# Attention, RWKV and feed-forward layer on one core: new opening, rings and order, clamps on ScalarE, one product for gain and row scale, and sums as accumulating DMAs

## What is computed

```python
x = x + attention(ln(x))          # q = h @ W_q.T; (q @ h.T) @ h, no softmax
x = x + ffn(ln(x))                # f1
x = x + rwkv(ln(x))
x = x + ffn(ln(x))                # f2, the same weights

def ffn(t):                       # the router's weight is 1 for expert 0
    z = t + relu(t @ w1 + b1) @ w2 + b2
    return ln(z) * gamma + beta

def rwkv(x):
    xa = ln(x) * g1 + b1n; xx = shift(xa)                 # shift: one token later
    k, v, r = (mix of xa and xx with mix_k, mix_v, mix_r) @ Wk, Wv, Wr
    x = x + (sigmoid(r) * wkv(decay, first, k, v)) @ Wo   # a running maximum, two running sums over tokens
    xc = ln(x) * g2 + b2n; xx2 = shift(xc)
    kv = square(relu(mix(xc, xx2) @ FWk)) @ FWv
    return x + sigmoid(mix(xc, xx2) @ FWr) * kv
```

## Time and profile before

| | |
|---|---|
| median of 3 runs | 297.18 us (295.85 to 297.45) |
| the profiled execution | 295.44 us, span 293.6 us |
| TensorE busy | 264.2 us (90% of the span) |
| VectorE busy | 246.4 us (84%) |
| ScalarE busy | 218.7 us (74%) |
| GpSimd busy | 141.2 us (48%) |
| mean granted TensorE clock | 0.973 |

### The profile page before, as it was taken

The page is one execution under the profiler, slowest core; times in us unless marked ns, Lnnn a source line. Parts: engine busy times, 40 slices in busy tenths (PEclk is TensorE's granted clock), DMA queues, the critical chain, the costliest instruction groups (busy, mean ns, idle before and its releaser), DMA issues.

```text
span 293.6 us, 5283 instructions
## 1 busy us (share of the span) xinstructions
PE 264.2 (90%) x1538; PEld 192.0 (65%) x1538; DVE 246.4 (84%) x776; ACT 218.7 (74%) x427; POOL 141.2 (48%) x273
## 2 busy tenths in 40 slices
PE   5378999999999997499899999899999988999990
PEld 5376776678677677266666675696477564867760
DVE  1478369999999999889999999999999999883233
ACT  2369759865999494859999969739979597778630
POOL 1547659725990555726227025637476244431311
PEclk9599999999999999789999999999999999999998
DMA  6921310202220031131022204101400222403031
GB/s 178 300 52 31 60 23 1 36 0 38 36 40 0 0 54 21 17 69 24 1 37 38 36 0 74 36 1 20 90 1 2 36 36 36 112 1 74 0 71 36
DMA packets 14716, 12.59 MB, mean 43 GB/s; under 512 B 1120, under 2 KB 11232, under 8 KB 14688
## 3 DMA queue, kind: packets, MB, share of 16 engines
q0 software_dynamic: 3456, 6.29, 12.6%
q1 hardware_dynamic: 11232, 5.97, 7.1%
HBM read 3.87 MB, written 2.10 MB: 20 GB/s over the span
## 4 chain that ended last, share of the span: by engine, by line
PE 40%; DVE 24%; ACT 12%; issue 12%; POOL 5%; SPq 3%; DMA 2%; POOLq 0%; DVEq 0%; ACTq 0%
PE bank L898 10%; PE bank L883 9%; PE bank L940 6%; PE bank L946 4%; DVE R L383 2%; PE bank L844 2%; ACT KK L738 2%; DMA R<-in_hidden 2%; PE bank L957 2%; PE bank L928 2%; ACT N L632 1%; ACT NC L632 1%; DVE f_zn_stats L332 1%; DVE tmix_stats L332 1%; PE bank L890 1%
## 5 line engine op out<-in xcount | busy, mean ns | idle before, releaser
L898 PEld LDWEIGHTS bank<-W,f_h 128*128 128x128 f32 x512 | 60.1, 192 | 6.6 <-ACT f_h L692 3.5
L898 PE MATMUL bank<-W,f_h 128*128 128x128 f32 x512 | 62.7, 276 | 0.8 <-ACT f_h L692 0.8
L883 PE MATMUL bank<-f_yT,W 128*128 128x512 f32 x128 | 62.0, 601 | 0.7 <-ACT f_yT L684 0.7
L692 ACT ACTIVATE f_h<-bank,B1C 128x512 f32<-128x512 f32 x64 | 42.5, 681 | 14.7 <-PE bank L883 13.4
L946 PEld LDWEIGHTS bank<-FWv,KK 128*128 128x128 f32 x256 | 31.0, 192 | 6.9 <-ACT KK L742 3.1
L883 PEld LDWEIGHTS bank<-f_yT,W 128*128 128x128 f32 x128 | 21.8, 190 | 19.7 <-issue 13.5
L940 PE MATMUL bank<-XK,FWk 128*128 128x512 f32 x64 | 32.4, 620 | 0.6 <-DVE XK L507 0.5
L946 PE MATMUL bank<-FWv,KK 128*128 128x128 f32 x256 | 31.9, 276 | 0.6 <-ACT KK L742 0.5
L632 ACT ACTIVATE f_y<-R,f_yn_nb,f_yn_rs 128x128 f32<-128x128 f32 x64 | 26.3, 486 | 4.6 <-POOL f_yn_nb L252 4.6
L247 POOL TENSOR_TENSOR f_yn_ve<-f_yn_mv,K_EPS 128x4 f32<-128x4 f32 x16 | 4.5, 282 | 43.4 <-DVE f_yn_mv L360 43.4
L297 POOL DMA_DIRECT2D R<-BETA x16 | 15.4, 963 | 20.5 <-ACT f_y L632 20.2
(11 more groups left out here) (131 smaller groups left out, 610.2 us busy)
## 6 DMA issues: line engine op xcount, KB each, us to landing
R<-BETA POOLq DMA_DIRECT2D x16, 256.0 KB, 3.4
R<-in_hidden SPq DMA_DIRECT2D x8, 256.0 KB, 5.0
R<-N POOLq DMA_DIRECT2D x8, 256.0 KB, 3.4
out_x<-R SPq DMA_DIRECT2D x8, 256.0 KB, 2.3
W<-in_w SPq DMA_DIRECT2D x2, 256.0 KB, 3.1
BETA<-in_beta SPq DMA_DIRECT2D x1, 256.0 KB, 4.4
FWk<-in_f_wk SPq DMA_DIRECT2D x1, 256.0 KB, 3.7
FWv<-in_f_wv SPq DMA_DIRECT2D x1, 256.0 KB, 4.8
```

The costliest lines, as they stand in the source:

```text
L692: a.activation(f.h[:, n, :], banks[bank][:], ACT.Relu, bias=B1C[:, n:n + 1]).then_inc(f.h_ready[n], 1)
L883: t_.matmul(banks[bank][:], W1[:, n * P:(n + 1) * P], f.yT[b % Y_COPIES][:], start=True, stop=True).then_inc(f.h_psum[n], 1)
L898: last = t_.matmul(banks[bank][:, j * C:(j + 1) * C], f.h[:, n, j * P:(j + 1) * P], W2[:, n, :], start=False, stop=(n == H - 1), skip_grou ...
```

## The change

Everything that VectorE, ScalarE, GpSimd and TensorE do per batch stays, except for these parts.

- The clamps of the exponents go from VectorE to ScalarE, as Relu of x and Relu of -x; the second exponential gets scale -1.
- `ffn_gain` and `ffn_out` are replaced. `ffn_scaled` computes zg = (z x row scale) x GAMMA in one instruction per row group, out of PSUM, once the power is there. zg is then added to R: by `ffn_sum`, an accumulating DMA from GpSimd, or for batch 0 of f1 and batch 7 of f2 by `ffn_add` on VectorE.
- `cmix_out` becomes `cmix_sum`, an accumulating DMA, for batches 0 to 6. Batch 7 stays on VectorE.
- With the beta sum, the sum of N, and these, each batch has up to five accumulating DMAs, three of them new.
- Tiles become rings: XN 3 copies, XNT, GRAM and PROJ 2, N 3, zg 3; the rest as before.
- `scale`, `scale_only`, `scale_twice` and `back_scale` on GpSimd are split into their steps (`shift`, `power`, `bias`, ...), which its list interleaves. The number of their instructions is the same.
- The opening: another order of loads, 42 warm-up transposes, `decay_rates` behind the first two normalisations instead of ahead of them, and the attention of batches 0 to 6 largely ahead of the first `hidden_up`.
- All four lists are new.

```diff
-WARM_UP = 24
-N_COPIES = 2
-Y_COPIES = 2
+COPIES = {"N": 3, "f1_y": 2, "f2_y": 2, "f1_yT": 2, "f2_yT": 2, "XN": 3, "XNT": 2, "GRAM": 2, "PROJ": 2, "f1_zg": 3, "f2_zg": 3, "others": 1}
+ADDED = {"f1": (0,), "f2": (7,), "x3": (7,)}
...
             load_x0(0)
+            load_x0(1)
             sp.dma_start(Wq[:], w_q).then_inc(first_loaded, DMA)
             sp.dma_start(VEC[:], vectors).then_inc(first_loaded, DMA)
+            load_x0(2)
+            sp.dma_start(B1[:], b1).then_inc(w1_loaded, DMA)
             sp.dma_start(W1[:], w1).then_inc(w1_loaded, DMA)
-            sp.dma_start(B1[:], b1).then_inc(w1_loaded, DMA)
+            load_x0(3)
             sp.dma_start(W2[:], w2.rearrange("(f p) c -> p f c", p=P)).then_inc(w2_loaded, DMA)
-            load_x0(1)
+            load_x0(4)
...
+            def ffn_sum(b, f, tile):
+
+                pool.wait_ge(f.zg_ready, b + 1)
+                pool.wait_ge(*f.xb.ready(b))
+                if b >= 2:
+                    pool.wait_ge(*f.out.ready(b - 2))
+                pool.dma_start(R[b][:], at(tile, b)[:], accum_op=ALU.add).then_inc(*f.out.step(b))
+
+            def cmix_sum(b):
+
+                pool.wait_ge(*cgate.done(b, "kvs"))
+                pool.wait_ge(*x2u.ready(b))
+                if b >= 2:
+                    pool.wait_ge(*x3.ready(b - 2))
+                pool.dma_start(R[b][:], at(G2, b)[:].rearrange("p (j c) -> p j c", j=J), accum_op=ALU.add).then_inc(*x3.step(b))
...
-            def ffn_gain(b, f, bank):
+            def ffn_scaled(b, f, bank):
...
                 dve.wait_ge(f.z_psum, b + 1)
-                v.tensor_tensor(f.zg[:], bank_rows(bank), GAMMA[:].unsqueeze(1).broadcast_to([P, J, C]), ALU.mult).then_inc(f.zg_ready, 1)
...
                 dve.wait_ge(*f.znorm.scale.done(b, "rs"))
+                if b >= len(f.zg):
+                    dve.wait_ge(*f.out.ready(b - len(f.zg)))
+                z, zg = bank_rows(bank), at(f.zg, b)
+                for j in range(J):
+                    last = v.scalar_tensor_tensor(zg[:, j, :], z[:, j, :], f.znorm.rs[b % 2][:, j:j + 1], GAMMA[:], ALU.mult, ALU.mult)
+                last.then_inc(f.zg_ready, 1)
+
+            def ffn_add(b, f, tile):
+
                 dve.wait_ge(f.zg_ready, b + 1)
-                for j in range(J):
-                    last = v.scalar_tensor_tensor(R[b][:, j, :], f.zg[:, j, :], f.znorm.rs[b % 2][:, j:j + 1], R[b][:, j, :],
-                                                  ALU.mult, ALU.add)
-                last.then_inc(f.out_ready, 1)
+                dve.wait_ge(*f.xb.ready(b))
+                v.tensor_tensor(R[b][:], at(tile, b)[:], R[b][:], ALU.add).then_inc(*f.out.step(b))
...
+            def exponents_high(b):
+                act.wait_ge(*expo.done(b, "diff"))
+                if b >= len(EB):
+                    act.wait_ge(m1_ready, b - len(EB) + 1)
+                a.activation(at(EB, b)[:], at(EA, b)[:, 0:3:2, :], ACT.Relu).then_inc(expo.sem(b), 1)
+
+            def exponents_low(b):
+
+                act.wait_ge(*expo.done(b, "high"))
+                a.activation(at(EA, b)[:, 0:3:2, :], at(EA, b)[:, 0:3:2, :], ACT.Relu, scale=-1.0).then_inc(expo.sem(b), 1)
```

More of the change, by code:

```diff
@@ L577, in _ @@
-            mean_var(3, nt); exponents_low(1); cmix_change(0); cmix_k(0); z_stats(4, f1, 2); cmix_r(0)
-            mean_var(4, f1.znorm); ffn_gain(4, f1, 2); tmix_change(2); first_values(1, 3); mix_k(2); mix_v(2)
-            ffn_out(4, f1); mix_r(2); tmix_stats(4); cgate_log(0, 6); new_values(1, 3); denominator_sum(1)
-            numerator_sum(1); mean_var(4, nt); weighted(1); cmix_gated(0, 2); with_current(1); cmix_out(0)
-            gate_sum(1); ffn_stats(0, f2); gate_log(1, 7); mean_var(0, f2.norm); running_max(2, 2); gated(1)
@@ new lines, in _ @@
+            z_stats(1, f1, 3); mean_var(1, f1.znorm); attn_out(4, 5); ffn_stats(4, f1); mean_var(4, f1.norm)
+            ffn_scaled(1, f1, 3); tmix_change(0); mix_k(0); mix_v(0); mix_r(0); running_max(0, 1); differences(0, 1)
+            tmix_stats(1); mean_var(1, nt); z_stats(2, f1, 5); mean_var(2, f1.znorm); new_values(0, 1)
+            denominator_sum(0); numerator_sum(0); first_values(0, 1); weighted(0); ffn_scaled(2, f1, 5)
+            with_current(0); tmix_change(1); gate_sum(0); mix_v(1); mix_k(1); gate_log(0, 7); tmix_stats(2)
@@ new lines, in _ @@
+            z_stats(3, f1, 4); gated(0); running_max(1, 0); mean_var(2, nt); tmix_out(0, 2); differences(1, 0)
+            cmix_stats(0); mean_var(3, f1.znorm); mean_var(0, ncm); mix_r(1); attn_out(5, 0); ffn_stats(5, f1)
+            mean_var(5, f1.norm); new_values(1, 3); ffn_scaled(3, f1, 4); denominator_sum(1); first_values(1, 3)
+            numerator_sum(1); z_stats(4, f1, 7); cmix_change(0); weighted(1); cmix_k(0); with_current(1); cmix_r(0)
+            gate_sum(1); tmix_stats(3); mean_var(4, f1.znorm); mean_var(3, nt); gate_log(1, 6); attn_out(6, 0)
@@ L623, in _ @@
+            ffn_add(7, f2, f2.zg)
         @block.scalar
@@ L870, in attn_apply @@
                 for j in range(J):
-                    last = t_.matmul(banks[bank][:, j * C:(j + 1) * C], XNT[:, j * P:(j + 1) * P], PROJ[:], start=True, stop=True)
+                    last = t_.matmul(banks[bank][:, j * C:(j + 1) * C], at(XNT, b)[:, j * P:(j + 1) * P], at(PROJ, b)[:], start=True, stop=True)
                 last.then_inc(attn_psum, 1)
```

902 lines of the change are left out of this document (453 added, 449 removed).

## The result

The changed kernel takes 285.1 us (median of four runs, 283.48 to 286.37) beside 296.56 us (295.85 to 297.45) for the kernel before in the same session: a ratio of 0.961, 95% interval 0.954 to 0.968, so 3.9% faster. Forecast were 284.5 us in 275 to 295. The profiled execution took 286.06 us with a span of 284.3. The close agreement of the medians therefore hides an error of 3.4 us in the spans, and that error has two parts of opposite sign, as the windows show.

The account below looks back on a forecast made before the run. VectorE was taken to bound the kernel, 97.7% busy from 60 to 240 us. Span 293.6 - 1.3 - 5.5 - 6.0 + 0.1 = 280.9; + 1.84 = 282.7 profiled; + 1.74 = 284.5 us median, range 275 to 295.

Parts of the forecast that it names:

- The opening: Up to the first feed-forward matmul: 1.3 us shorter, 26.1 instead of 27.38, with 5.5 us of TensorE work moved into it.
- everything behind moves by 3.9 us: Opening: mean_var(0) directly behind the first statistics runs at 4.5 instead of 8.37, so ScalarE starts about 6.6, TensorE 7.9.
- The clock in the opening: Opening: 18 added warm-up transposes cover TensorE's idle time and keep the first attention batches at 2.4 GHz.
- The middle: Between first feed-forward matmul and last matmul: 6.0 us from closed holes and clock, besides 5.5 us of work moved out.
- three quarters of 7.9: Middle: of 7.9 us lost to one accident of VectorE's queue (holes 5.4, clock 2.5), 6.0 us are regained.
- The sizes: Work moved between engines: VectorE loses 25.5 us to 221, ScalarE gains 16.9 to 235.6, GpSimd goes from 141.2 to 161.
- The tail: After the last matmul: 0.1 us longer; power 0.6 us earlier, four products as before, then ffn_add with 0.68.
- Rival 1: Middle: all TensorE holes close, gaining 14.9 instead of 6.0 us, span 272.0, time 275.5; chance 0.22.
- the 14.8 of the range: Middle: the favourable end, -14.8 us, all 12.3 us of TensorE idle and the clock's loss regained.
- Rival 2: Middle: ScalarE becomes the limit, filled to no more than 83%; middle 260.8 us, time 297.5, no change; chance 0.06.
- Rival 3: DMA sums: 7 of 21 land 2.6 us late each, costing 18 us, time 302.6; chance 0.12.
- Nothing is exposed at the measured latency, by 0.3 us: DMA sums: 4.4 us from issue to landing, issue included, stays hidden behind shortest VectorE covers of 4.7 us.

Follow-up runs that it names:

- e1: The changed kernel run again unaltered, as the yardstick for the other runs: 283.51 us, ratio 0.957 to the kernel before.
- e2: The changed kernel with centre_down_bias moved on VectorE from behind mean_var(0) to behind mean_var(3): 281.55 us, ratio 0.953 to the kernel before.
- e10: The changed kernel with clamps (directly behind differences), gain and scale, and all sums but the attention's back on VectorE; opening, rings and order kept: 300.72 us.
- e8: The changed kernel with centre_down_bias behind mean_var(3) and the warm-up back at 24 transposes instead of 42: 281.16 us, ratio 0.950 to the kernel before.
- e3: The changed kernel with both clamps back on VectorE, directly behind the differences of their batch: 298.65 us, ratio 1.008 to the kernel before.
- e11: The changed kernel with both clamps back on VectorE, two calls further back than in e3: 293.53 us, ratio 0.992 to the kernel before.
- e6: The kernel before with only the clamps moved to ScalarE, each pair ahead of its batch's first exponential: 312.05 us, ratio 1.055 to the kernel before.
- e12: The changed kernel with one copy instead of three of the tile zg between product and sum: 285.04 us, ratio 0.962 to the kernel before.
- e4: The changed kernel with all 21 new accumulating DMA sums put on VectorE as single additions: 295.33 us, ratio 0.999 to the kernel before.
- e5: The changed kernel with the feed-forward's old separate gain and four scaled sums on VectorE, without ffn_sum DMAs: 287.66 us, ratio 0.970 to the kernel before.
- e9: The changed kernel with only the third sum of each batch (cmix_out) back on VectorE: 288.5 us, ratio 0.974 to the kernel before.

## Why the prediction was right, and where not

The time came out in the range and in the forecast direction, and the relief of VectorE in the middle was the right mechanism. That 284.5 and 285.1 lie so close is luck: the opening was 6.2 us too long, the middle 3.1 us too short, and the 1.74 us that the sum adds for the median came from only three executions.

**The opening: wrong.** Forecast were ScalarE at 6.6 (measured 6.86), the first transpose at 7.9 (9.00), and the first up matmul at 26.1; it came at 32.26, and at 28.35 in e1. The count of work done by then was exact: 183 instructions instead of 119, of which 18 are warm-up and 46 attention, as summed. The step that failed is "everything behind moves by 3.9 us": the prediction counted ScalarE's queue as the longest and did not ask what stood behind `centre_down_bias` on VectorE, nor what `centre_bias` stands behind on TensorE. It also wrote that the added transposes "end at 8.9 at worst, 1 us after the first tile is there", at "cost 0". The size was right (9.02); the dependant was missed. Without the wait the up matmul comes at 27.12 (e2), 1.0 us behind the forecast. From there 1.2 us lead to e1's 28.35 at clock 1.00, and the other 3.9 to 32.26 are the slower warm-up (1.3) and the lower clock (2.6), as e1 shows. The forecast had no term for either. In the median e2 puts the cost of the wait at 2.0 us. The error in the profiled execution is +6.2 us; with -3.1 in the middle (244.67 against 247.7 forecast) and +0.3 in the tail that makes the 3.4 of the span.

**The clock in the opening: an incomplete argument.** TensorE had worked since 1.53, yet after a pause of 3.01 us the clock was 0.56 from 13 to 20 us; in e1 a pause of 2.78 us ahead of the same transpose left it at 1.00 from 8 to 27. The other executions with the call in its old place side with these two: in six more the pause was 3.02 us and the clock from 13 to 20 us was 0.57 to 0.80, in e10 it was 2.49 us and the clock stayed at 1.00. The Trainium skill ("TensorE: Matmul & The Clock Gate", What's actually happening), by which activity releases the fast clock, agrees in direction with the first. What sets how long the clock stays low after the same pause was not found. In e8 the clock from 8 to 14 us was lower than in e2 and the first up matmul no later.

**The middle: the right length, but a thin reason.** Forecast were 239 us of TensorE work and 8.7 of idle; measured are 236.99 and 7.7, at clock 1.00, so -14.6 us instead of -11.5. The price "three quarters of 7.9" came from one accident in VectorE's queue. The runs show a broader cause: with all moves undone VectorE is busy over 99% from 80 to 220 us, and the moves are worth 17.2 us for 22.2 us of VectorE's busy time (e10 against e1). For the order with its rings no gain of its own is shown: e10, which has the new opening too, is 4.7 us slower than before, of which up to 5 us may be the placing of the clamps (e3 against e11). That the order is what lets ScalarE's longer chain run without stopping VectorE is argued from e6, where the clamps alone cost 16 us; e6 has one placing only.

**The sizes** of the moved instructions were right (see above), and the busy totals of VectorE and ScalarE wrong by overlap. GpSimd's forecast was 12.5 us too high.

**The tail:** 0.4 instead of 0.1. The scaled sum of before is now a product and an addition, as forecast.

**Rival 1, all holes close, 275.5** (its sum has 14.9 for the 14.8 of the range)**:** did not come. VectorE is still busy 137.4 of 140 us from 80 to 220 in the profile of the changed kernel. I had divided its share over the whole middle (82%) and called that slack. The best version here, e8, is at 281.16.

**Rival 2, ScalarE takes VectorE's place:** no. ScalarE is busy 164.48 of 180 us, above the 83% that the rival named as its filling, and the middle did not lengthen. It was a wrong bound: ScalarE reached 91%, and 94% from 80 to 220 us.

**Rival 3, late DMA sums:** no. "Nothing is exposed at the measured latency, by 0.3 us" holds: both new kinds land after 3.4 us although the queue's share doubled from 12.6% to 24.3%, VectorE waits for them for 0.3 us in total and ScalarE for 0.6, and e12 shows that even one tile would do. The Trainium skill ("DMA: Bandwidth & Descriptors", Anatomy of one DMA — SWDGE (gpsimd) path) gave an estimate of 2.6 us by its formula; the traces of both kernels disagree, with 3.4.

## What to carry to other kernels

Where one engine is busy 97% or more for a long stretch, price what is taken from it by its own time in that stretch, and not by the holes that it leaves on the engine behind it. Here a us of VectorE's was worth 0.7 to 1.0 us of the span behind the first up matmul (e4, e5, e9, e10, e11), and 0.5 to 1.1 by medians. Before the work is put on an in-order engine with slack, look where the result is read, and let only what the reader needs stand ahead of it: the same move gave 10 us in the new order and cost 16 in the old. And when a queue's head is lengthened (a warm-up, here), list every engine that waits for something behind it.

## What was not expected

The same 42 transposes took between 6.16 and 7.74 us from one execution to the next, at a granted clock of 1.00 from 0 to 8 us in each, and 24 took 4.23 to 5.18. They run at two rates: 6 or 7 begin or run in each us at first, 11 or 12 later, and what varies is the moment between. In e10 it lies between 4 and 5 us, in the changed kernel at about 7. TensorE alone from 5 to 6 us, e10 and then the changed kernel (busy us, instructions, granted clock, DMA share, GB/s):

```profile
5.00:6.00 1.00, 1.00 (x12) 1.00 0.95 234
...
5.00:6.00 1.00, 1.00 (x6) 1.00 0.99 246
```

The granted clock does not tell the two apart, and what sets the moment stays open. The spread of the changed kernel's executions, 282.31 to 286.37 us, goes with it and with the clock behind the pause: at a mean granted clock of 0.994 and 0.995 they took 282.31 and 282.42 us, at 0.988 and 0.989 283.48 to 284.13, at 0.981 286.06 and 286.37.
Undoing the three moves singly costs more (24.3 us, with the clamps placed alike) than undoing them together (17.2). Why was not tested.
